# The masked attention's stacked rows in 49 direct transfers instead of 12 through a scratch, with edits of order in three layers

## What is computed

```python
x = x + masked_attention(layernorm(x), ctx)   # 32 query heads, 8 key groups of 16 features
x = x + ternary_ffn(layernorm(x))             # rounded activations, ternary weights
x = x + sequence_attention(layernorm(x), ctx) # 8 heads over the sequence
x = x + gated_ffn(layernorm(x))               # 512 -> 2 x 2048 -> 512
```

```python
q = q.reshape(b, LQ, G, HPG, HD).transpose(0, 2, 3, 1, 4)
k = k.reshape(b, LKV, G, HD).transpose(0, 2, 1, 3)
scores = jnp.einsum('bgrqd,bgkd->bgrqk', q, k) / jnp.sqrt(jnp.float32(HD))
scores = jnp.where(causal_mask[None, None, None, :, :], -jnp.inf, scores)
scores = jnp.where(padding_mask[:, None, None, None, :], -jnp.inf, scores)
w = jax.nn.softmax(scores, axis=-1)
```

## Time and profile before

| what | us |
|---|---|
| time, median of 3 runs | 1662.22 (1661.37 to 1663.94) |
| time of the profiled execution | 1662.86 |
| its span, first to last instruction | 1661.0 |
| PE busy | 1398.8 (84%) |
| DVE busy | 792.2 (48%) |
| ACT busy | 723.3 (44%) |
| POOL busy | 490.8 (30%) |

### The profile page before, as it was taken

How to read it: one execution, slowest core, us unless ns; L and a number is a source line. 1 busy time by engine, 2 the same in 40 slices (tenths; PEclk the granted TensorE clock), 3 DMA queues, 4 the chain that set the end, 5 groups by cost and what they waited for, 6 DMA issues and landing times. The chain is left out here.

```text
span 1661.0 us, 22233 instructions
## 1 busy us (share of the span) xinstructions
PE 1398.8 (84%) x8324; PEld 664.8 (40%) x8402; DVE 792.2 (48%) x1278; ACT 723.3 (44%) x1356; POOL 490.8 (30%) x523
## 2 busy tenths in 40 slices
PE   4686686776766688888589999998999999999998
PEld 3353453453442244544212222223444444444443
DVE  6564364463454378775376666652640320320220
ACT  2265465454555477777335556564430220220220
POOL 7211011153544566767322222214540000000000
PEclk9598898898888799999869999998999999999999
DMA  6626535536434201011353444323332001000000
GB/s 163 146 91 158 133 96 154 130 88 148 113 90 122 77 13 39 33 45 46 95 151 108 133 126 133 105 90 114 113 103 70 7 1 49 27 0 25 26 0 26
DMA packets 89285, 140.66 MB, mean 85 GB/s; under 512 B 8265, under 2 KB 47753, under 8 KB 88657
## 3 DMA queue, kind: packets, MB, share of 16 engines
q1 hardware_dynamic: 76384, 114.16, 25.1%
q10 hardware_dynamic: 12800, 25.17, 4.8%
HBM read 105.85 MB, written 33.46 MB: 84 GB/s over the span
## 5 line engine op out<-in xcount | busy, mean ns | idle before, releaser
L849 DVE TENSOR_REDUCE a_negmax<-a_psX 128x4 f32<-128x1024 f32 x128 | 151.6, 1217 | 152.6 <-PE a_psX L1065 152.6
L1647 DVE TENSOR_REDUCE c_negmax<-c_psA 128x1 f32<-128x512 f32 x256 | 165.8, 682 | 89.3 <-PE c_psA L1712 87.9
L1980 PE MATMUL d_psGU<-d_zt_hi,d_w_hi 128*128 128x512 bf16 x502 | 191.6, 382 | 3.0 <-ACT d_silu L1913 2.4
L1980 PE MATMUL d_psGU<-d_zt_lo,d_w_hi 128*128 128x512 bf16 x501 | 191.5, 382 | 2.3 <-DVE d_zt_lo L1932 1.8
L1980 PE MATMUL d_psGU<-d_zt_hi,d_w_lo 128*128 128x512 bf16 x501 | 191.4, 382 | 0.6
L1913 ACT ACTIVATE d_silu<-d_psGU 128x512 f32<-128x512 f32 x64 | 38.2, 596 | 348.9 <-PE d_psGU L1980 348.9
L722 ACT ACTIVATE a_probs<-a_psB 128x512 f32<-128x512 f32 x256 | 138.4, 595 | 117.6 <-PE a_psB L1077 111.7
L1605 ACT ACTIVATE c_probs<-c_psB 128x512 f32<-128x512 f32 x256 | 140.2, 595 | 109.2 <-PE c_psB L1725 109.2
L1943 DVE TENSOR_TENSOR d_h<-d_psGU,d_silu 128x512 f32<-128x512 f32 x64 | 44.2, 691 | 223.7 <-PE d_psGU L1980 223.4
L1065 PE MATMUL a_psX<-a_ks,a_qs 113*128 113x256 bf16 x512 | 82.8, 309 | 75.6 <-DMA a_qs<-q_scr 61.4
L630 POOL TENSOR_SCALAR ternary<-a_tern_stage 128x512 bf16<-128x512 f32 x48 | 91.9, 1928 | 138.5 <-ACT a_tern_stage L710 138.2
(11 more groups left out here) (222 smaller groups left out, 2507.3 us busy)
## 6 DMA issues: line engine op xcount, KB each, us to landing
a_tern_stage<-in_w ACTq DMA_DIRECT2D x32, 768.0 KB, 4.8
d_weight_stage<-in_w_last SPq DMA_DIRECT2D x24, 512.0 KB, 3.9
a_ks<-k_scr SPq DMA_DIRECT2D x8, 768.0 KB
a_qs<-q_scr SPq DMA_DIRECT2D x8, 768.0 KB
c_ks<-k_scr SPq DMA_DIRECT2D x48, 128.0 KB, 2.6
c_qs<-q_scr SPq DMA_DIRECT2D x48, 128.0 KB, 3.0
a_xz<-in_x SPq DMA_DIRECT2D x32, 128.0 KB, 7.3
a_ctx<-in_ctx_t SPq DMA_DIRECT2D x8, 512.0 KB, 8.9
```

Source lines behind the costliest of these rows:

```text
L849: v.tensor_reduce(negm[:, u, :], X[:, 2 * (u % 2):2 * (u % 2) + 2, :].rearrange("p a (j k) -> p (a j) k", k=SEQ), AX.X, ALU.max, negate=Tr ...
L1647: v.tensor_reduce(negm[:, u:u + 1], A[:, u % 2, :], AX.X, ALU.max, negate=True)\
L1980: last = pe.matmul(GU[:, 2 * up + i % 2, :], wgu[wh][:, i, up, k, :], zt[zh][:, k, :], start=(k == 0 and j == 0), stop=(k == DC - 1 and j ...
```

## The change

1. `stack(n)` has no scratch. The keys of each group go straight from their 16 partitions to the stack's rows, 24 transfers of 16 x 4 x 256 elements (the source is read four times over); the queries in 24 of 16 x 1024; with the padding row, issued first, 49 transfers. They count on `stacked[par]` (`STACKED` = 49). For the queries SP waits for both halves.
2. ACT writes `k_hi` and `q_hi` of batch n only when the whole stack of batch n-1 has landed (`stacks_through`).
3. `MAXES` goes from (0, 2, 2, 2, 2, 2, 3, 3) to (0, 0, 2, 2, 3, 3, 3, 3), `THIRDS` from (0, 2, 1, 2, 2, 1, 2, 2) to (0, 1, 1, 2, 2, 2, 2, 2).
4. The two pairs of banks of the units change places, so the transposes of xz wait for 15 maxima, and the key projection for the sixteenth.
5. In a group `out_high` stands ahead of the thirds on ACT, `out_low` ahead of the reductions on DVE, and a third unit behind `turn` on PE and behind `normalise` on DVE.
6. Ternary FFN: PE's last `down` of a tile goes behind the next turn's first two products; ACT takes h's slice 2 ahead of its fourth `gate`; DVE updates x behind its first `gate`.
7. Sequence attention: the first maxima wait for the first of two memsets, and DVE takes the statistics of batch 1 behind the first quad.

```diff
-    THIRDS = (0, 2, 1, 2, 2, 1, 2, 2)
+    THIRDS = (0, 1, 1, 2, 2, 2, 2, 2)
-    MAXES = (0, 2, 2, 2, 2, 2, 3, 3)
+    STACKED = 6 * GROUPS + 1
+    MAXES = (0, 0, 2, 2, 3, 3, 3, 3)
...
             def stack(n):
                 par = n % 2
                 if n:
-                    sp.wait_ge(stacked[1 - par], ((n - 1) // 2 + 1) * 3 * DMA)
-                sp.wait_ge(s["k_hi"], n + 1)
-                for copy in (0, 2):
-                    sp.dma_start(io["k_scr"][copy].rearrange("p g t -> g p t"), k_hi[:]).then_inc(s["k_out"], DMA)
...
-                sp.wait_ge(s["q_out"], (n + 1) * 6 * DMA)
-                sp.dma_start(qs[par][R_HI:R_PAD].rearrange("p h t -> p (h t)"),
-                             io["q_scr"].rearrange("a p g n -> (a p) (g n)")).then_inc(stacked[par], DMA)
+                    sp.wait_ge(stacked[1 - par], ((n - 1) // 2 + 1) * STACKED * DMA)
...
+                for done, k, rows in (("k_hi", k_hi, (R_HI, R_LO)), ("k_lo", k_lo, (R_HI2,))):
+                    sp.wait_ge(s[done], n + 1)
+                    for row in rows:
+                        for grp in range(GROUPS):
+                            sp.dma_start(ks[par][row:row + HD, :, grp, :],
+                                         k[grp * HD:(grp + 1) * HD].rearrange("p (o t) -> p o t", o=1)
+                                         .broadcast_to([HD, QJ, SEQ])).then_inc(stacked[par], DMA)
+                for done, q, rows in (("q_hi", q_hi, (R_HI, R_HI2)), ("q_lo", q_lo, (R_LO,))):
+                    sp.wait_ge(s[done], 2 * n + 2)
+                    for row in rows:
+                        for grp in range(GROUPS):
+                            sp.dma_start(qflat[par][row:row + HD, grp * SHARE * SEQ:(grp + 1) * SHARE * SEQ],
+                                         q[grp * HD:(grp + 1) * HD].rearrange("p a j c i -> p (a j c i)"))\
+                                .then_inc(stacked[par], DMA)
...
+            def stacks_through(n):
+                if n:
+                    act.wait_ge(stacked[(n - 1) % 2], ((n - 1) // 2 + 1) * STACKED * DMA)
...
-                    need(act, s["k_out"], n * 3 * DMA)
+                    stacks_through(n)
...
-                        pe.wait_ge(s["max_done"], MU * (m + 1))
+                        pe.wait_ge(s["max_done"], MU * (m + 1) - 1)
...
-                down(t - 2, NF - 1)
+                    down(t - 3, NF - 1) if n == 0 else down(t - 2, n - 1)
...
-                front.statistics(dve, 1)
                 for quad in range(2):
                     maxima(0, quad, range(MQ))
                     split_max(0, quad)
+                    if quad == 0:
+                        front.statistics(dve, 1)
```

More of the change, by code:

```diff
@@ L444, in build_masked_attention @@
                  "xz_loaded ctx_loaded xr_loaded stats_done rstd_done shift_done z_ready ctx_split kv_proj "
-                 "k_hi k_lo v_ready zt_done zt_hi zt_lo q_proj q_hi q_lo k_out q_out stacked0 stacked1 max_units max_done "
+                 "k_hi k_lo v_ready zt_done zt_hi zt_lo q_proj q_hi q_lo stacked0 stacked1 max_units max_done "
                  "m_fix m_split mt_done mt_copied mt_out shift_loaded score_units exp_done pv_done os_copied turned "
@@ L687, in project @@
                 if n is not None:
-                    need(act, s["q_out"], n * 6 * DMA)
+                    stacks_through(n)
                     for half in range(2):
@@ L729, in attend @@
                     exponentials(b, 2 * g)
+                    if g in (3, 5, 7):
+                        out_high(b, (g - 3) // 2)
                     for k in behind[:1]:
@@ L868, in attend @@
                     units = list(range(sum(MAXES[:g]), sum(MAXES[:g + 1]))) if more else []
-                    for u in units[:1]:
-                        reduce_unit(b + 1, u)
                     if g in (3, 5, 7):
                         out_low(b, (g - 3) // 2)
-                    for u in units[1:]:
+                    for u in units[:2]:
                         reduce_unit(b + 1, u)
@@ L876, in attend @@
                         normalise(b, g - 1)
+                    for u in units[2:]:
+                        reduce_unit(b + 1, u)
                     if g == 3 and b + 2 < BATCH:
@@ L998, in project @@
                     pe.wait_ge(s["ctx_split"], 2 * (n + 1))
+                    if m is not None:
+                        pe.wait_ge(s["max_done"], MU * (m + 1))
                     if n == 0:
@@ L1054, in max_unit @@
                 if u == 0:
-                    pe.wait_ge(stacked[par], (n // 2 + 1) * 3 * DMA)
+                    pe.wait_ge(stacked[par], (n // 2 + 1) * STACKED * DMA)
                     need(pe, s["x_updated"], ST * (n - 1))
@@ L1103, in attend @@
                         score_unit(b, 2 * g + 2, 1)
-                    for u in units:
+                    for u in units[:2]:
                         max_unit(b + 1, u)
@@ L1107, in attend @@
                         turn(b, g - 1)
+                    for u in units[2:]:
+                        max_unit(b + 1, u)
                     if g + 1 < GROUPS:
@@ L1306, in _ @@
                     squares(t, 2)
+                take("h", t - 2, 2)
+                if now:
                     gate(t, 3)
-                take("h", t - 2, 2)
                 if 1 <= t <= NT:
@@ L1363, in _ @@
                 ahead = front.prepare(dve, t + RU) if t + RU < NT else iter(())
+                if now:
+                    gate(t, 0)
                 if t >= 3:
                     update(t - 3)
-                if now:
-                    gate(t, 0)
                 if 1 <= t <= NT:
@@ L1440, in _ @@
                             transposed("x", t + 1, j)
-                down(t - 2, NF - 1)
+            down(NT - 1, NF - 1)
 def build_sequence_attention(nc, io, keep, x_out, front, following):
@@ L1706, in maximum @@
                 at = MQ * (2 * n + quad)
+                if n == 1 and quad == 0 and u == 0:
+                    pe.wait_ge(s["init"], 2)
                 if u == 0:
```

26 lines of the change are left out of this document (5 added, 21 removed).

## The result

| what | before | after |
|---|---|---|
| median of 4 runs, us | 1661.80 | 1733.45 |
| span of the profiled execution | 1661.0 | 1732.4 |
| PE busy | 1398.8 | 1428.4 |
| ACT busy | 723.3 | 719.7 |

The ratio is 1.0431, with an interval of 1.0413 to 1.0449. The forecast was 1628 with a range to 1680, and the slow rival 1685; the kernel came out above both.

The account below looks back on a forecast made before the run. A loop of waits was taken to bound the masked attention, PE the ternary FFN. The terms, 0 - 22 - 0.8 + 4.5 + 5.3 - 20 - 3 = -36, rounded to -34, gave 1628 us, range 1606 to 1680.

Parts of the forecast that it names:

- slow rival: SP's issue queue is the new bound: both transfer kinds at 0.64 us, stack 7.7 us later in six batches, 1685; 20%.
- Term 1: Masked attention, stack transfers: 48 issues at a 0.475 us pitch replace the scratch round trip exactly, change 0.
- 0.573: Issue pitch in us at which the forecast's gain of 34 us is used up, at 347 us per us of pitch.
- Term 4: Kernel start: ACT's k_hi of batch 1 waits for batch 0's whole stack, +5.3 us; +15.6 at a 0.64 pitch.
- Term 2: Masked attention: six groups instead of seven behind the stack's wait, -22 us, batch 0 -0.8; order inside groups counted 0.
- Term 3: Masked attention, batches 4 to 7: ACT's second-last third waits about 1.5 us for POOL's roundings in three batches, +4.5 us.
- Term 5: Ternary FFN: PE's two waits a tile go, a tile takes 13.5 us instead of 14.97, -20 us over 14 full tiles.
- rival with 14.97 kept: Ternary FFN: ACT or DVE becomes its bound, a tile's 14.97 us stays within 0.3, total 1644; 10%.
- Term 6: Sequence attention: first reductions start 4.5 us earlier, batch 1's stack comes some 1.3 us too late, -3 us in all.
- test that the forecast named first: SP's issues of the two new lines in the later profile: 430 ns each if right, 590 to 600 for the rival.
- the three it named last: Signs of being wrong: SP stalls on full DMA rings, transfers land much later than 2 us, ACT's POOL waits reach several us a batch.

Follow-up runs that it names:

- e2: Kernel before with items 1 and 2 alone (49 direct transfers, ACT's wait for the whole stack): 1729.02 us, ratio 1.0409.
- e10: Kernel before with only the queries in 24 direct transfers, the keys still through the scratch: 1660.61 us, ratio 0.9994.
- e6: Changed kernel with the stack through the scratch again and all of item 5 undone: 1640.03 us, ratio 0.9871 against the kernel before.
- e1: Changed kernel with the stack through the scratch again, all else of the change kept: 1663.36 us against 1661.34 for the kernel before, ratio 1.0008.
- e11: Changed kernel, 49 transfers included, with out_high on ACT back behind the thirds and the results: 1709.43 us, ratio 1.0291 against the kernel before.
- e7: Kernel before with item 7, and ACT copying the first quad's maxima ahead of batch 1's z: 1666.31 us, ratio 1.0033.
- e9: Kernel before with item 7, ACT's copy of quad 0's maxima and SP's shift of them both moved ahead: 1660.18 us, ratio 0.9991.
- e8: Kernel before, unchanged, plus a block behind its end timing groups of six back-to-back transfers by memories and rows: 1744.38 us, 84 of it the block's own.

## Why the prediction was wrong

**Term 1, the pitch, is the step that failed.** "I take 0.475, since it is of the same kind (stack rows, plain, issued back to back)": the row was of another kind, a load from DRAM. Measured: 0.635 to 0.648, so +48 (e2) to +50 us in six batches where the term said 0. The slow rival had this case at 0.64 with +46, and was given 20%; its mechanism and its number of 7.7 us a batch (7.9 in batch 2) held. The trace before had no issue within SBUF at all. In this layer most of its issues took 0.56 to 0.63: the writes of k and q to the scratch, the padding row, the loads and the stores of x. The 0.43 came from another layer. With no row of the right kind, and the whole result hanging on 0.573, that bore 50 to 20 badly. The Trainium skill's "DMA: Bandwidth & Descriptors", section "Rules for kernel authors" ("Coalesce into one large transfer"), came out on the right side, and through the issue alone: the 2.0 us of each transfer ran beside the others, and 48 times 0.16 us more was enough. With 24 such transfers e10 lost nothing.

**Term 4, the start**, hung on the same number: +5.3 forecast, 14.9 measured, 15.6 at the rival's pitch. ACT wrote k_hi of batch 1 at 56.72, in the moment stack 0 had landed (rival: 56.5):

```profile
56.72 0.47 ACT L684 ACTIVATE a_k_hi<-a_psX,bk 128x256 bf16<-128x256 f32 x1 [19.90 <-DMA a_qs<-a_q_lo]
```

**Term 2, one group less behind the wait, was right in mechanism and size, and item 5 hid it.** -22.8, with POOL's +4.5 -18, against the -17 that remain for items 3 and 4 in e6. In e1, with item 5 in place, nothing of it is left.

**Item 5 was counted at nothing; it costs some 23.** "So I count 0 and keep up to -10": the part on DVE and PE does give some 7, but out_high on ACT costs 30 (24 beside the long stack). The term looked at how full ACT is and not at what it waits for: out_high needs a turn back that PE makes behind its weighing, and moved ahead of the second pair of exponentials it makes these wait for it too, and PE for these, 1.57 us in two groups of each of the batches 2 to 7; and behind the first of them the clock falls back to 1.2 GHz for some 3 us. This is the part that no rival had, and why the time is above the 1685 of the slow one: 1685 + 23 (item 5) + 11 (FFN) + 8 (sequence attention) = 1727, against 1733. With the 24 that e11 measured for out_high in place of 30 it is 1721; the 6 to 12 us that are left belong to no term that a run has apart.

**Term 3, POOL**: the stalls stood in batches 4 and 5 before the change as well, 8.3 us in group 5 instead of 5.4; in e6 they are in the last group instead. ACT's waits for POOL's rounding went from 5.8 us to 9.1 in e6, 3.3 more where the term had 4.5; no run measures the term alone, and in the changed kernel they are 1.3.

**Term 5, the FFN**: right mechanism, half the size, -9.1 instead of -20. "I take 13.5" holds for every other tile, where PE's two waits of the earlier trace rows go; the tile between takes 15.2, since ACT is late in it with x's rounding and with slice 2. The rival with 14.97 kept is wrong too.

**Term 6, the sequence attention**: wrong sign, +5.4 instead of -3. The term followed the moved statistics over POOL's z to SP's stack, and missed what else stood behind z: on ACT the copy of quad 0's maxima, on SP their shift. e7 and e9 show both; each alone hides the other.

**What held**: the stack's wait is still PE's longest, the landing is 2 us, and no issue waited for data. The test that the forecast named first, issues at 590 to 600 ns, was the one that decided; the three it named last (full rings, late landings, ACT's waits for POOL) were not seen.

## What to carry to other kernels

When a design trades a few large transfers for many small ones on one queue, the price is the issue: count them, and take its time from a row with the same source and target memories and the same form; between SBUF and SBUF it was 0.635 us here, and the whole decision hung on 0.573. Without such a row, time six issues first, as e8 does. Before an instruction is moved ahead on an in-order engine, ask what it waits for and who waits behind it; a busy share says nothing of that. And where two waits lie one behind the other, as ACT's copy and SP's shift here, mending one shows nothing: read the next queue before the edit is given up.

## What the runs showed of the hardware

The time of one issue on SP is longer within SBUF than for the same plain rows from or to DRAM: six back to back of 16 rows of 2 KB took 585 ns each within SBUF, 420 from DRAM, 420 to DRAM, and for 128 rows 606, 432 and 451 (e8). Other forms between DRAM and SBUF also took about 0.6 us: a load of 64 rows, all on partitions 64 to 127, 596 (e8), the writes of k_hi to the scratch 620, the padding row 630 (kernel before). What makes these long, and why issues within SBUF take longer at all, stays open. The first issue after a pause took 303 to 349 ns between DRAM and SBUF (488 for the 64 rows); within SBUF the first was not always the shortest (487 to 730).

PE's granted clock, once at 2.4 GHz after a long wait, did not always stay there. In the changed kernel PE idled 1.57 us soon after the rise, and the clock was at 1.2 GHz again for some 3 us behind it, in all six batches that wait for their stack. In e11, with the same long wait and without that idling, it stayed up in all six.
